# Local-attention layers: units of four heads instead of pairs, scores in row halves, one exponential per unit, head norms behind the rotation

## The reference, cut to what matters

```python
for i in range(6):
    x = attn_layer(shift_tokens(x), Wqkv[i], ...) + x      # 16 heads of 64
    x = ffn_layer(shift_tokens(x), ...) + x
# attn_layer:
q = l2norm(q) * qs;  k = l2norm(k) * ksc                   # per head
q = q * cos * scale + rotate_half(q) * sin * scale
k = k * cos / scale + rotate_half(k) * sin / scale
# local_attention: token i sees keys i-32 .. i
attn = softmax(q k^T * 8 + mask);  out = attn @ v
```

## Time and profile before

| | |
|---|---|
| runs | 5981.24, 6000.6, 6007.14 us; median 6000.6 |
| profiled execution | 6004.01 us; its span 6002.2 us |
| granted TensorE clock, mean | 0.89 of full |
| busy share of the span | PE 87%, DVE 68%, ACT 43%, POOL 13% |
| local stage | from 608.5 us (first L1617) to some 2.71 ms, six layers; the third takes 348.6 us |

### The profile page before, as it was taken

How to read it: one execution, slowest core, us unless ns; L and a number is a source line. 1 busy time by engine, 2 the same in 40 slices (tenths; PEclk the granted TensorE clock), 3 DMA queues, 4 the chain that set the end, 5 groups by cost and what they waited for, 6 DMA issues and landing times. The chain is left out here.

```text
span 6002.2 us, 67570 instructions
## 1 busy us (share of the span) xinstructions
PE 5247.9 (87%) x19735; PEld 2604.6 (43%) x19735; DVE 4108.1 (68%) x6066; ACT 2587.5 (43%) x4954; POOL 782.0 (13%) x702
## 2 busy tenths in 40 slices
PE   7888787978888797887978999999999999999994
PEld 2333453535445353543334444444444444444442
DVE  3666665647466564744647888888888888888875
ACT  1444553536455363641442444444444444444441
POOL 0000442424234242420010000000000000000000
PEclk7778888888888888885778999999999999999996
DMA  0000000000000000000000000000000000000000
GB/s 17 3 0 0 29 11 9 1 19 1 17 3 11 9 2 18 1 1 10 1 24 4 2 1 4 1 3 3 3 3 3 3 1 4 1 3 3 1 1 8
DMA packets 18045, 35.02 MB, mean 6 GB/s; under 512 B 3418, under 2 KB 12250, under 8 KB 16746
## 3 DMA queue, kind: packets, MB, share of 16 engines
q1 hardware_dynamic: 17642, 30.22, 1.6%
HBM read 29.69 MB, written 0.52 MB: 5 GB/s over the span
## 5 line engine op out<-in xcount | busy, mean ns | idle before, releaser
L1137 DVE TENSOR_REDUCE xat_part<-xat_ring 128x1 f32<-128x512 f32 (+1 forms) x1664 | 1086.8, 668 | 260.3 <-PE xat_ring L969 241.4
L1080 ACT ACTIVATE xat_p_full<-xat_sc 128x1024 f32<-128x1024 f32 (+1 forms) x816 | 835.2, 1024 | 963.3 <-PE xat_sc L1015 959.8
L1167 DVE TENSOR_TENSOR xat_p_sum<-xat_p_sum,xat_p_full 128x1024 f32<-128x1024 f32 x768 | 936.2, 1219 | 43.1 <-ACT xat_p_full L1080 35.6
L996 PE MATMUL xat_acc<-xat_p_full,xat_v 128*64 128x512 f32 (+1 forms) x3264 | 883.2, 619 | 1.3 <-ACT xat_p_full L1080 1.2
L969 PE MATMUL xat_ring<-xat_k_hl,xat_q_hh 128*128 128x512 f32 (+1 forms) x1664 | 717.0, 446 | 53.7 <-DVE xat_k_hl L1134 18.4
L1014 PE MATMUL xat_sc<-xat_q_hh,xat_k_hl 128*128 128x512 f32 (+1 forms) x1632 | 750.1, 460 | 0.0
L1015 PE MATMUL xat_sc<-xat_q_lm,xat_k_h 128*128 128x512 f32 (+1 forms) x1632 | 648.8, 398 | 0.0
L969 PEld LDWEIGHTS xat_ring<-xat_k_hl,xat_q_hh 128*128 128x128 f32 x1664 | 312.6, 189 | 709.4 <-issue 335.1
L1686 DVE TENSOR_REDUCE loc_peak<-loc_sc 128x2 f32<-128x320 f32 x384 | 188.3, 490 | 495.8 <-PE loc_sc L1434 492.2
L1536 ACT ACTIVATE loc_probs<-loc_sc,loc_peak 128x160 f32<-128x160 f32 x768 | 294.0, 387 | 501.0 <-DVE loc_peak L1686 493.4
L1593 POOL TENSOR_TENSOR loc_probs<-loc_probs,loc_rinv 128x320 f32<-128x320 f32 x384 | 353.3, 920 | 863.6 <-DVE loc_rinv L1691 860.2
(11 more groups left out here) (386 smaller groups left out, 7702.6 us busy)
## 6 DMA issues: line engine op xcount, KB each, us to landing
loc_w_qkv<-in_L_ffn_w SPq DMA_DIRECT2D x6, 1536.0 KB, 6.5
loc_w_o<-in_L_ffn_wo SPq DMA_DIRECT2D x6, 512.0 KB, 3.2
xat_ctxT<-in_ctxT SPq DMA_DIRECT2D x12, 256.0 KB, 2.7
xat_w_qk<-in_L_xattn_wqk SPq DMA_DIRECT2D x16, 128.0 KB, 2.0
loc_w<-in_L_ffn_w SPq DMA_DIRECT2D x6, 341.0 KB, 3.0
loc_w<-in_L_ffn_w SPq DMA_DIRECT2D x6, 192.0 KB, 2.4
loc_rope<-in_rope SPq DMA_DIRECT2D x1, 1024.0 KB
xat_w_o<-in_L_xattn_wo SPq DMA_DIRECT2D x16, 64.0 KB, 1.8
```

The costliest lines, as they stand in the source:

```text
L996: last = pe.matmul(acc[h * GROUP:(h + 1) * GROUP, e, :], v[0:size, t, e * GROUP:(e + 1) * GROUP], p_full[0:size, t % 3, cols(h)], start=(t ...
L1080: act.activation(p_full[0:size, j % 3, :].rearrange("p (a b) -> p a b", a=2), sc[0:size, x:x + 2, :], ACT.Exp, scale=GROUP ** -0.5).then_i ...
L1137: ins = dve.tensor_reduce(part[:, t, c:c + 1], ring[:, b, 0:chunks[c][1]], AX.X, ALU.max)
L1167: dve.tensor_tensor(p_sum[:, e, :], first_in, p_full[:, (j - 1) % 3, :], ALU.add)\
```

## The change

- A unit is four heads (two pairs); a layer has 32 units, each over two steps. `units(step)` replaces `pairs(step)`; the preparation keeps its places p.
- **Scores.** The mask product comes first, into two banks. Then four matmuls of 64 rows each (rows 0 to 63 one head, 64 to 127 the other) with 160 columns; `k_pair` becomes `kT`, without zeros. The tile `sc` holds one unit, so the next unit's scores wait for `sub_done`. `out_ps` holds one unit too.
- **Softmax.** DVE takes the four maxima, subtracts them from PSUM into `probs` (two instructions, 128 keys and 32 keys of each head apart), ACT takes one exponential of 640 elements in SBUF, DVE sums (two reductions, one addition), inverts, POOL multiplies in two instructions.
- **Transposes.** Four of 128 keys and one for the 32 extra keys of all four heads, which land on four groups of 32 partitions.
- **Output.** Eight matmuls: 64 columns of `v` as weights, 128 columns streamed, over 128 keys; then over 32 keys with `v_more` on the same groups of 32 partitions. ACT, no longer DVE, copies the result to `att`.
- **v.** Eight v products, and eight times a product "x" of the extra 32 tokens in four matmuls, each to its own 32 partitions; it waits until v has been copied out of `pr`.
- **Norms.** ACT copies `pr` to `qk` behind the square; DVE multiplies `pr` by cos directly and un-normalised; POOL makes the sin part and now also the addition (1024 elements); DVE multiplies by the inverse norm last, k at p=4, q at p=6. The next product waits for copy and cos.

The diff, cut to its core:

```diff
-        k_pair = s.sb("k_pair", [P, 3, LPAIRS, 2, SPAN])
-        probs = s.sb("probs", [P, 4, 2, SPAN])
+        kT = s.sb("kT", [P, 3, LPAIRS, SPAN])
+        probs = s.sb("probs", [P, 4, 4 * SPAN])
+        v_more = s.sb("v_more", [P, 3, 4, LDIM])
...
+            return {-4: ([("k", t)], []), -1: ([("q", t)], []), 2: ([("v", t)], []), 3: ([("x", t)], []), 6: ([], ["k"]), 7: ([], ["q"])}
...  # PE, prepare
+                        if kind in "qv":
+                            pe.wait_ge(S["copy_done"], i * (2 * NTOK) + (kind_at("vq".index(kind), u) + 1))
+                            pe.wait_ge(S["cos_done"], i * (2 * NTOK) + (kind_at("vq".index(kind), u) + 1))
+                        elif kind == "x":
+                            pe.wait_ge(S["v_done"], i * (2 * NTOK) + (2 * u + 1))
+                            for n in range(4):
+                                cols = w_qkv[:, 2 * LINNER:].rearrange("p (u r e) -> p r u e", r=4, e=LDIM)
+                                last = pe.matmul(pr[n * WIN:(n + 1) * WIN, 0:4 * LDIM],
+                                                 xs[:, (u + 1) * P:(u + 1) * P + WIN], cols[:, head_of[n], :, :], ...)
...  # PE, units
+                    if step % 2 == 0 and x < UNITS:
...
+                        if x:
+                            pe.wait_ge(S["sub_done"], i * UNITS + x)
+                        for odd in range(2):
+                            pe.matmul(sc[:, odd, 0:2 * SPAN], ident_bf[:], band_bf[:, min(t, 1), :, :], ...)
+                        for c in range(2):
+                            for odd in range(2):
+                                rows = slice(64 * odd, 64 * odd + 64)
+                                last = pe.matmul(sc[:, odd, c * SPAN:(c + 1) * SPAN], qT[rows, t % 2, 2 * u + c, :],
+                                                 kT[rows, t % 3, 2 * u + c, :], ...)
...
+                        for c in range(4):
+                            last = pe.transpose(tr[:, n % 2, c * P:(c + 1) * P], probs[:, x % 4, c * P:(c + 1) * P], g.ident[:])
...
+                        pe.transpose(tr[:, n % 2, 0:P], probs[:, x % 4, 4 * P:4 * SPAN], g.ident[:])
...
+                                pe.matmul(to, v[:, t % 3, head * LDIM:(head + 1) * LDIM],
+                                          pT[:, x % 2, n * P:(n + 1) * P], start=True, stop=False, ...)
...
+                                last = pe.matmul(to, v_more[rows, t % 3, u, :], pT2[rows, x % 2, :], ...)
...  # ACT, prepare and units
                         act.activation(sind[:, w, :], pr[:], ACT.Square).then_inc(S["sq_done"], 1)
+                        act.activation(qk[:, w, :], pr[:], ACT.Copy).then_inc(S["copy_done"], 1)
...
+                    if step % 2 == 0 and x < UNITS:
+                        act.wait_ge(S["sub_done"], i * UNITS + (x + 1))
+                        act.activation(probs[:, x % 4, :], probs[:, x % 4, :], ACT.Exp).then_inc(S["exp_done"], 1)
...
+                        act.activation(att[:, 2 * u:2 * u + 2, t * P:(t + 1) * P],
+                                       out_ps[:, :, 0:P],
...  # POOL, prepare at p = 0 (k) and p = 3 (q)
+                    pool.tensor_tensor(cosd[:, w, :], cosd[:, w, :], sind[:, w, :], ALU.add)\
...  # DVE, prepare
+                        dve.tensor_tensor(heads(cosd[:, w, :]), heads(pr[:]),
                                           tab[:, 2 * w, t, :].unsqueeze(1).to_broadcast([P, LHEADS, LDIM]), ALU.mult)\
...
+                    if p == -2:
+                        times_cos(1)
...
+                    if p == 1:
+                        times_cos(0)
                         sum_squares(0)
...
+                    if p == 4:
                         normalise(1)
+                    if p == 6:
                         normalise(0)
...  # DVE, units
+                        dve.tensor_reduce(most, got, AX.X, ALU.max, negate=True).then_inc(S["max_done"], 1)
...
+                            last = dve.tensor_tensor(to, got[:, :, :, first:first + width],
+                                                     most.unsqueeze(3).to_broadcast([P, 2, 2, width]), ALU.add)
+                        last.then_inc(S["sub_done"], 1)
```

More of the change, by code:

```diff
@@ L1366, in local_stage @@
         pr_at, tr_at = {}, {}
-        for step in range(-NP - 4, PAIRS + 4):
-            if 0 <= step - 3 < PAIRS:
-                tr_at["p", step - 3] = len(tr_at)
+        for step in range(-NP - 4, STEPS + 8):
+            if step % 2 and 0 <= step - 3 < STEPS:
+                for kind in "pe":
+                    tr_at[kind, (step - 3) // 2] = len(tr_at)
             for t, p in preparing(step):
@@ L1378, in local_stage, with attention @@
         kind_at = lambda w, t: 2 * t + 1 - w
-        def attention(pairs, prepare):
-            for step in range(-NP - 4, PAIRS + 6):
+        def attention(units, prepare):
+            for step in range(-NP - 4, STEPS + 8):
                 if step >= 0:
-                    pairs(step)
+                    units(step)
                 for t, p in preparing(step):
@@ L1445, in pairs @@
[L1445 to L1457, removed]
@@ new lines, in units @@
+                    x = (step - 4) // 2
+                    if step % 2 == 0 and 0 <= x < UNITS:
+                        t, u = divmod(x, UN)
+                        pe.wait_ge(S["tr_free"], i * (TR * NTOK) + (tr_at["e", x] + 1))
+                        if x:
+                            pe.wait_ge(S["o_free"], i * UNITS + x)
+                        if u == 0:
+                            pe.wait_ge(S["v_done"], i * (2 * NTOK) + (2 * t + 2))
+                        for c in range(2):
+                            for odd in range(2):
+                                n = 2 * odd + c
+                                to = out_ps[64 * odd:64 * odd + 64, c, 0:P]
+                                head = 4 * u + 2 * c + odd
+                                pe.matmul(to, v[:, t % 3, head * LDIM:(head + 1) * LDIM],
+                                          pT[:, x % 2, n * P:(n + 1) * P], start=True, stop=False,
+                                          skip_group_check=True)
+                        for c in range(2):
+                            for odd in range(2):
+                                n = 2 * odd + c
+                                rows = slice(n * WIN, (n + 1) * WIN)
+                                to = out_ps[64 * odd:64 * odd + 64, c, 0:P]
+                                last = pe.matmul(to, v_more[rows, t % 3, u, :], pT2[rows, x % 2, :],
+                                                 start=False, stop=True, skip_group_check=True)
+                        last.then_inc(S["o_ps"], 1)
@@ L1529, in prepare @@
[L1529 to L1541 removed]
+                            keys = tr[:, x % 2, :].rearrange("p (c q) -> p c q", q=P)
@@ new lines, in prepare, with units @@
+                            last = act.activation(kT[:, t % 3, 4 * b:4 * b + 4, WIN:SPAN], keys, ACT.Copy)
+                            if t < NTOK - 1:
+                                last = act.activation(kT[:, (t + 1) % 3, 4 * b:4 * b + 4, 0:WIN],
+                                                      keys[:, :, P - WIN:P], ACT.Copy)
+                            last.then_inc(S["tr_free"], 1)
+                def units(step):
+                    x = step // 2
+                    if step % 2 == 0 and x < UNITS:
+                        act.wait_ge(S["sub_done"], i * UNITS + (x + 1))
+                        act.activation(probs[:, x % 4, :], probs[:, x % 4, :], ACT.Exp).then_inc(S["exp_done"], 1)
+                    x = (step - 3) // 2
+                    if step % 2 and 0 <= x < UNITS:
@@ L1542, in pairs @@
                         n = tr_at["p", x]
                         act.wait_ge(S["tr_ps"], i * (TR * NTOK) + (n + 1))
-                        act.activation(pT[:, x % 2, :], tr[:, n % 2, 0:2 * P], ACT.Copy)
-                        act.activation(pT2[:, x % 2, :], tr[0:WIN, n % 2, 2 * P:4 * P], ACT.Copy)\
-                           .then_inc(S["tr_free"], 1)
-                attention(pairs, prepare)
+                        if x >= 2:
+                            act.wait_ge(S["o_ps"], i * UNITS + (x - 1))
@@ L1549, in _ @@
+                attention(units, prepare)
                 norm.scalar(act, i)
@@ L1601, in _ @@
                 layer(i)
+                pool.wait_ge(S["add_done"], i * (2 * NTOK) + 2 * NTOK)
                 pool.wait_ge(S["cos_done"], i * (2 * NTOK) + 2 * NTOK)
```

219 lines of the change are left out of this document (105 added, 114 removed).

## The result

The changed kernel takes 5826.1 us (median of 4 runs, 5810.0 to 5828.9) where the kernel before, run beside it, took 6003.9; ratio 0.9706, 95% interval 0.9675 to 0.9736. The forecast was 5850. The profiled execution's span is 5822.9 us. From the first to the last instruction on its tiles the local stage took 1930.5 us for 2121.2, so 191 us less; all other stages together took 11 us more in this one execution of each, in the same code, and no run says why.

The account below looks back on a forecast made before the run. PE was taken to bound the blocks, with one hole and its half-rate aftermath. Seven blocks 15.4, last block 7, start 3: 25.4 us a layer, 152 over six layers, from 6004 to 5850 us; range 5700 to 6010.

Parts of the forecast that it names:

- Last block: A layer's last block, without preparation: 21.4 us, 23 with slow stretches, against 29.8; 7 us gained (4 to 8.5).
- Start: Start of a layer: one v product and a short one replace two, sin starts earlier; 3 us gained (0 to 5).
- The legs: Block walked at full clock between exponentials' ends at p = 0, 2, 4, 6: 6.95, 7.8, 4.3, 8.45; sum 27.5 us.
- charge for half rate: PE at half rate behind its gap ahead of "x": scores and "x" 1.2 us, following PE work about 2.1.
- one hole that the sums don't give: Today's block: PE sits 3.18 us for ACT once, then runs at half rate; cited for the more-waits rival.
- The two cos products beside POOL: DVE's cos products reading PSUM beside POOL: 0 to 1.08 us on the first leg, taken as 0; other end 45 us.
- Changes of shape on PE: PE tile shape changes: 0.5 us a unit taken; at 0.15 each, five cost 0.75, taking 12 us from the gain.
- More waits: Rival: the in-order walk misses waits; blocks stay at 33 us, only both ends gain 10; 5945 us, chance 0.16.
- clock stays low: Rival: PE with narrow tiles, waiting for DVE, never regains full clock; block 37.4 us, 6170 in all; chance 0.15.
- no overlap: Rival: narrow products don't run side by side in PE's array; block 34.5 us, about 6005 in all; chance 0.07.
- Clock holds: Rival: no slow stretch on PE; block 27.5 us, 52 us a layer gained, 5690 in all; chance 0.12.
- POOL never waited for: Sign that the forecast is right: no engine waits for POOL; transposes waiting for POOL would show it wrong.

Follow-up runs that it names:

- the order alone: Kernel before with only the norm moved behind the rotation; copies and additions stay on DVE, pairs as before: 5876.4 us, ratio 0.9787.

## Why the forecast was right, and where it wasn't

**The sum.** Local stage: forecast 152 us less, measured 191; 11 of the 39 us between them are hidden in the total by the other stages, which is chance. Block 31 forecast, 29.4 measured (2.2 x 7 = 15.4 became 3.9 x 7 = 27.3, the block before being 33.3). Last block 7 forecast, 6.8. Start 3 forecast, about nothing. Tail "unchanged", 2 lost: `w_o`'s 32 instructions take 16.07 us for 13.97, as PE comes to them from the gaps of a last block that is no longer full.
```profile
1501.29 16.07 PE L1496 MATMUL loc_pr<-loc_att,loc_w_o 128*128 128x512 f32 x32 [0.59 <-ACT loc_att L1581]
```
32 us a layer, six layers 191.

**The legs**, from one exponential's end to the next, in us:

| leg | forecast, full clock | measured, third layer |
|---|---|---|
| 0 to 2 | 6.95 | 6.72 to 6.81 |
| 2 to 4 | 7.8 | 7.85 in the block at clock 0.94, else 8.8 to 9.2 |
| 4 to 6 | 4.3 | 4.1 to 6.1 |
| 6 to 0 | 8.45 | 8.53, once 7.63 |
| charge for half rate | 3.3 | 0 to 2.8 over the shortest block (27.8), mean 1.6 |
| last block, a unit | 3.85 | 3.85 |

The walk of the changed kernel held: two legs in every block, the other two in the shortest. The charge was twice what it is, though the shortest block itself has a clock of 0.94, so that some half rate is counted in its legs. What the walk missed is the 2.42 us wait for the single `out_ps`.

**The step that failed** is the attribution. The prediction took PE's work, from 26.0 to 17.3 us a block, as what the change removes, and priced the norms at "nothing" and the moved copies as within the legs. The runs show the reverse: the new preparation alone is worth 191 us, the units alone minus 19. The range was met for a reason that the prediction doesn't give: I walked the *changed* kernel, preparation included, and compared with the measured block of before: a difference of two totals needs no attribution. Had I walked the old preparation with units, or the new with pairs, the split would have shown. Three things hid it. The hole of the earlier trace rows was taken as a given of the old block ("one hole that the sums don't give") and not followed through ACT to a maximum 3.5 us late on DVE. The spread of L1640, 1224 to 2296 ns, was read for what cos would cost after, not for what the norms and cos cost before. And a saving on the bound engine (true: 3.4 us less PE work took 2.6 us off a block) was counted as the gain of the units, though with the new preparation the next chain stands 0.3 us below PE, and with the old one the units' own chain takes 34.2 us.

**Single prices.** The two cos products beside POOL were taken at no loss against an upper end of 1.08: all 96 of L1684 lie between 1212 and 1226 ns, and 48 of them ran beside a POOL instruction. These rows agree with the Trainium skill, VectorE: DVE Perf Modes, section Two Vector instructions with no wait between them, by which the second of two SBUF inputs is read over an interface shared with GpSimd. L1640 before, with two SBUF inputs, shows the other side: the 48 of 96 that ran beside POOL took 2.28 us, the other 48 took 1.22, and the median of 1752 ns is a time that none of them took. With POOL's sin cut short 82 of the 96 ran beside nothing and the median is 1224. The changed kernel gains here twice: cos reads `pr`, and 77 of its 96 norms (L1690) ran beside nothing, at 1.21 to 1.23 us.

Changes of shape on PE: by the prediction's estimate from the Trainium skill, TensorEngine Tiling (Array Packing), section Tiling Modes, they would have taken another 12 us. Three of a unit's five shapes (scores, output, extra keys) take 0.75 + 0.59 + 0.37 us, where full overlap gives 0.53, 0.43 and 0.21: 0.54 us more in these three alone, against 0.5 for all five in the sum and 0.75 in the estimate. What part is draining and what is incomplete overlap, no run parts.

**Rivals and signs.** "More waits" (33 us a block) and "clock stays low" (37.4) are out by the blocks of 29.4 us, "no overlap" by the run without row halves. "Clock holds" (5690) isn't true of any block, as none has a clock above 0.94; 11 of 42 still take 27.6 to 27.8 us, near its 27.5. Of the signs, the first two row halves start 0.01 us apart (1390.19 and 1390.20), and DVE's maximum waits for PE in 116 of 192 units. "POOL never waited for" failed by little: PE's transposes waited for it 20 times, 16 us in all.

## What to carry to other kernels

Follow a hole back to the instruction that was late, through every engine, before you count the work around it: here it led to two DVE products that took 2.3 us instead of 1.2 beside POOL. A preparation in which they no longer meet was worth 190 us (132 by its order alone), while the units, which take some 6 us of work a block from the busiest engine (26.7 shown busy against 21.0, at clocks of 1.00 and 0.94), were worth none. Walk a change of several parts once for each part as well as for the whole. And when the engine that bounds a loop is to be relieved, first work out how far below it the next chain stands.

## What was not expected of the hardware

- DVE products of two SBUF inputs beside POOL's: 2.28 us, and 1.22 alone (L1640 before, 48 of each); at most 3.09 in the kernel with the extra values in their own bank (L1700: 1214/1365/3091 ns over 96). With a PSUM input: none of 96 over 1.226 (L1684 after), 48 of them beside POOL.
- A hole's length doesn't settle the granted clock of its block. Before, most blocks with one hole of 3.18 us had 0.85 and took 34.2 us, but four had 0.95 and took 31.2 to 31.5. With the order alone, 32 blocks with a hole of 1.44 us had 0.94 (26 of them took 30.8 or 30.9 us) and four had 1.00 (29.2 us).
- Two column halves of one pair gained little: 4 instructions of 128 columns, 0.43 us one after another, took 0.37 from start to start; in a unit, 8 took 0.59, and the 8 on four row groups 0.37.
- Small instructions suffer too, and by which POOL instruction runs beside them: the bound on 32 elements took 0.18 us alone and 0.32 beside L1593 (L1668 before), and 0.90 or more in all 48 cases after (L1705), 42 of them beside L1638. An addition of 128x4 elements took 0.16 us alone and 1.42 beside POOL's addition (L1747 at 1409.94, extra values in their own bank).
